# The offsets' 3x3 convolution in five matmuls a piece, with the third taps of two rows in one

## The chip, the cores and the metric

The kernel runs on one core of one Trainium2 chip. The metric is the device time of one execution in microseconds (us), as the median of several runs.

## What is computed

The input is 8 images of 64 channels and 16 x 16 pixels. Two residual blocks follow one another; the second is where the change lies.

```python
x = x + _L0_conv_ref(_gn(x), ...)      # 3x3 average pool, local 3x3 attention, gate, projection
x = x + _L1_conv_ref(_gn(x), L1_conv_w_om, L1_conv_b_om, L1_conv_w_dcn)

def _L1_conv_ref(x, w_om, b_om, w_dcn):            # DG, K = 4, 3
    om = conv_general_dilated(x, w_om, (1, 1), ((1, 1), (1, 1))) + b_om   # 3x3, 64 -> 108 channels
    o1, o2, mask = jnp.split(om, 3, axis=1)
    offset = jnp.concatenate([o1, o2], axis=1)
    mask = jax.nn.sigmoid(mask)
    return jax.nn.relu(_mdcn(x, offset, mask, w_dcn))   # bilinear samples at 9 shifted taps, x mask, x w_dcn
```

`_gn` is a group norm over pairs of channels. The convolution that is changed is `om`: for each pixel and each of nine taps it gives, for four channel groups, a mask and an offset in y and in x.

## The kernel before

**Layout.** Two halves of four images each lie on the partitions: half 0 on partitions 0 to 63 (64 channels), half 1 on 64 to 127, and along the free axis four images of 256 pixels. The first block (attention) fills the time to about 53 us; then come the second group norm's statistics, the convolution for the offsets, and the sampling, which runs over 72 steps (8 images x 9 taps).

**The convolution.** For each half there is a buffer, `dup[0]` and `dup[1]`, with four images padded to 18 x 18. Its lower 64 partitions hold the image, its upper 64 the same image moved by one column. So one matmul over 128 rows does two of the three taps of a row of the 3 x 3 stencil (kx 0 and 1), and another, with zero weights in the upper half, does the third (kx 2). With three rows that makes `TAPSTEPS` = 6 matmuls for a piece. There are five pieces: pieces 0 and 1 are one image slot each (256 columns, fp32), pieces 2, 3 and 4 two slots each (512 columns); pieces 0 to 2 read half 0, pieces 3 and 4 half 1. `convolve(p, k)` (L1139) issues step k of piece p; the last step signals `s_conv`.

**After a piece.** ACT's `offsets(p)` (L563) adds the bias (L568) and takes a tanh of the mask rows (L570). DVE's `offset_part` cuts the result into three bf16 parts (L849 to L857), and DMAs from SP (and for piece 0's x rows from POOL, L436) bring the parts to the stacks. From the stacks PE chooses rows: `select_y` (L1200), `select_x` (L1214), the masks (L1183, L1189). ACT makes distances and hats from these (L591, L596, L604, L606), DVE and POOL the low parts of the y hats (`low_y`), PE spreads them (L1229), DVE multiplies (L888) and PE takes the products (L1255).

**Order around the convolution.** Each engine has one hand-written order. DVE writes `dup[0]` image by image (L682, eight instructions, `s_dup0`), then `tall` (four, `s_tall`), a taller copy of all images from which the sampling windows are staged (`stage`, L834). PE does all of pieces 0 and 1 and three steps of piece 2, the first choices and windows, the rest of piece 2 between them, then the sampling. There, in image 0, each of the taps 0 to 5 carries one step of piece 3, and in image 3 taps 4 and 5 carry four and two steps of piece 4. ACT does `offsets(0)`, `second_half` (L555: two copies that fill `dup[1]` from `tall`), `offsets(1)`, then a queue of distances, hats and window copies up to `offsets(2)` (L626 to L636). POOL clears buffers at the start, works for the attention, issues the three DMAs of L436, and does `low_y` for the sampling. SP issues the loads of all constants at the start, the convolution's weights `womt` (L346) as the fourth.

Of the kernel before, what the change touches and what calls it, by code (L numbers as in the profile page):

```python
# [5 lines left out]
B, C, H, W = 8, 64, 16, 16  # L6
# [31 lines left out]
CHUNKS = 3  # L38
TC = TAPS // CHUNKS
CONV = [0, 1, 2, 3]  # L40
TAPSTEPS = 6
POOL_TAPS = 3


# [64 lines left out]
def bass_local_attention_then_deformable_conv(nc, x, cf, wom, sel16, rows16, out):  # L109
# [8 lines left out]
    with ExitStack() as ctx:  # L118
# [3 lines left out]
        def sem(name):  # L122
            return ctx.enter_context(nc.semaphore(name))
# [56 lines left out]
        window_words = sb("windows_attention", [P, max(len(PAIRROWS) * P + 2 * MSLOT, sum(n for _, n in ATT))])  # L180
        v = views(window_words, *ATT)
        pooled, q, chans, hidden, counts, shares, kpad, hsum, gate, att, vpad, dlog, lmax, den = (v[k] for k, _ in ATT)
        v = views(window_words, ("xs", len(PAIRROWS) * P), ("masks", 2 * MSLOT))
        xs, masks = v["xs"], v["masks"]

# [105 lines left out]
        s_dve = sem("s_dve")  # L291
        s_x2, s_x2seq = sem("s_x2"), sem("s_x2seq")
        s_tall, s_dup0, s_dup1 = sem("s_tall"), sem("s_dup0"), sem("s_dup1")
        s_conv, s_omraw, s_om, s_parts = (sem(n) for n in ("s_conv", "s_omraw", "s_om", "s_parts"))
        s_stack = {k: [sem(f"s_{k}stack{n}") for n in range(len(PIECES))] for k in "xym"}
        s_amaxed = sem("s_amaxed")
# [44 lines left out]
        @block.sync  # L341
        def _(sp):
            for c in range(2):
                sp.dma_start(xin[:, c * BANK:(c + 1) * BANK], x[:, c * BANK:(c + 1) * BANK]).then_inc(s_x[c], 16)
            sp.dma_start(bcast[:, 2 * DG * P:], sel16["bcast"][:, 3 * DG * P:]).then_inc(s_bcast, 16)
            sp.dma_start(womt[:, :], wom).then_inc(s_wom, 16)  # L346
            sp.dma_start(selx[:, :].bitcast(u16), sel16["selx"]).then_inc(s_selxd, 16)
            sp.dma_start(bcast[:, 0:2 * DG * P], sel16["bcast"][:, DG * P:3 * DG * P]).then_inc(s_byd, 16)
            sp.dma_start(sely[:, :].bitcast(u16), sel16["sely"]).then_inc(s_sel, 16)
            for k in range(3):  # L350
                for a in range(2):
                    sp.dma_start(selm[:, k * P + a * C:k * P + (a + 1) * C].bitcast(u16).rearrange("p (d c) -> p d c", d=DG),
                                 mask_columns(sel16["selm"], 3 * a + k)).then_inc(s_sel, 16)
                sp.dma_start(selm[:, 3 * P + k * C:3 * P + (k + 1) * C].bitcast(u16).rearrange("p (d c) -> p d c", d=DG),
                             mask_columns(sel16["selm"], 6 + k)).then_inc(s_sel, 16)
            for k in "xym":
                sp.dma_start(stack[k][STACK:STACK + 2, :].bitcast(u16), rows16["x" if k == "x" else "y"]).then_inc(s_rows, 16)

            sp.wait_ge(s_x2, 2)
            for h in range(HALVES):  # L360
                sp.dma_start(x2seq[:, :].rearrange("c (j h n) -> c j h n", j=J, h=HALVES)[:, :, h, :],
                             images(x2)[h * C:(h + 1) * C]).then_inc(s_x2seq, 16)

            for p, piece in enumerate(PIECES):
                for i in range(3):
                    sp.wait_ge(s_parts, 3 * p + i + 1)
                    sp.dma_start(*sent("y", piece, i)).then_inc(s_stack["y"][p], 16)
                for i in range(3):
                    if p:
                        sp.dma_start(*sent("x", piece, i)).then_inc(s_stack["x"][p], 16)  # L370
                for i in range(3):
                    if p:
                        whole = (piece[0], 0, BANK)
                        sp.dma_start(*sent("m", whole, i)).then_inc(s_stack["m"][p], 16)
            for i in range(B):
                sp.wait_ge(s_y, i + 1)
                sp.dma_start(in_order(out, i), result[:, i * HW:(i + 1) * HW]).then_inc(s_out, 16)
            sp.wait_ge(s_out, 16 * B)
            sp.wait_ge(s_choice, 1)
            passes = sp.value_load(choice[0:1, 0:1], min_val=1, max_val=SHIFTS)  # L380
            with sp.If(passes > 1):
                for i in range(B):
                    sp.wait_ge(s_y, B + i + 1)
                    sp.dma_start(in_order(out, i), result[:, i * HW:(i + 1) * HW]).then_inc(s_out, 16)
                sp.wait_ge(s_out, 2 * 16 * B)

        @block.gpsimd
        def _(pool):
# [4 lines left out]
            nc.gpsimd.memset(wb[:, :], 0.0).then_inc(s_wzero, 1)  # L393
            nc.gpsimd.memset(dup[0], 0.0).then_inc(s_zero, 1)
            nc.gpsimd.memset(dup[1], 0.0).then_inc(s_zero, 1)

            pool.wait_ge(s_zero, 6)
            pool.wait_ge(s_eps, 1)
# [35 lines left out]
            for i in range(3):  # L434
                pool.wait_ge(s_parts, i + 1)
                pool.dma_start(*sent("x", PIECES[0], i)).then_inc(s_stack["x"][0], 16)  # L436

            def stage(j, shift):

# [40 lines left out]
        def _(act):  # L480
# [70 lines left out]
            for c in range(2):  # L551
                high, _ = parts_at(c)
                nc.scalar.copy(halves[c][high, TAPS * HF:], den[high]).then_inc(s_rhi, 1)

            def second_half():  # L555

                act.wait_ge(s_tall, J)
                act.wait_ge(s_zero, 6)
                source = images(tall)[C:P, :, -FIRST_ROW * W:(-FIRST_ROW + H) * W].rearrange("p j (r c) -> p j r c", r=H)
                nc.scalar.copy(shifted(dup[1], 4)[0:C], source).then_inc(s_dup1, 1)  # L560
                nc.scalar.copy(shifted(dup[1], 3)[C:P], source).then_inc(s_dup1, 1)
# [46 lines left out]
            def sampling(it):  # L608
                for t in range(T):
# [13 lines left out]
                    if (i, m) == (LAST_CONV, 5) and isinstance(it, int):  # L623
                        offsets(4)

            offsets(0)  # L626
            second_half()
            offsets(1)
            distance_y(0, 0, 0)
            hat_x(0, 0)  # L630
            window_out(0, 0, 2)
# [367 lines left out]
        def _(pe):  # L999
# [139 lines left out]
            def convolve(p, k):  # L1139

                n, lo, hi = PIECES[p]
                h, j = n // 2, n % 2 * 2 + lo // HW
                ky, single = divmod(k, 2)
                if k == 0:
                    if h == 0:
                        pe.wait_ge(s_dup0, n % 2 * 2 + hi // HW)
                    else:
                        pe.wait_ge(s_dup1, 2)
                ins = nc.tensor.matmul(bank(CONV_BANK[p])[0:OM, lo:hi], womt[:, k * OM:(k + 1) * OM],  # L1149
                                       shifted(dup[h], 3 * ky + 2 * single)[:, j:j + (hi - lo) // HW], start=(k == 0),  # L1150
                                       stop=(k == TAPSTEPS - 1), skip_group_check=True)
                if k == TAPSTEPS - 1:
                    ins.then_inc(s_conv, 1)
# [169 lines left out]
            def sampling(it):  # L1323
                for t in range(T):
# [26 lines left out]
                    if i == LAST_CONV and m in (4, 5) and isinstance(it, int):  # L1351
                        if m == 4:
                            pe.wait_ge(s_vals, VALS * i)
                        for n in range(4) if m == 4 else (4, 5):
                            convolve(4, n)
                    if m in SEL_Y and i + 1 < B:
                        bank7_free(i, m, it)
# [20 lines left out]
                    block_of_products(B - 1, *LATE[m], it)  # L1378
                final(B - 1, it)

            pe.wait_ge(s_wom, 16)
            for p in range(2):
                for k in range(TAPSTEPS):
                    convolve(p, k)
# [18 lines left out]
            pe.wait_ge(s_absy, 2)  # L1403
            select_y(0, 2, 0)
            convolve(2, 4)
            convolve(2, 5)
            windows_out(0, 0)
            windows_out(1, 0)
            pe.wait_ge(s_wfin, 8)
# [124 lines left out]
```

## Time and profile before

| | us |
|---|---|
| median of 3 runs | 203.86 (203.85 to 203.88) |
| the profiled execution | 204.06 |
| its span on the core | 202.1 |

| engine | busy us | share of the span | instructions |
|---|---|---|---|
| PE (matmul) | 180.4 | 89% | 1806 |
| DVE | 160.8 | 80% | 268 |
| ACT | 106.5 | 53% | 199 |
| POOL | 84.6 | 42% | 103 |

Busy time counts an engine's instructions, not its waits for semaphores. The granted clock of TensorE was 0.998 of full over the execution. All times below are from the start of the span.

### The profile page before, as it was taken

The numbers are of one execution on the slowest core, as the hardware profiler recorded it, in microseconds if no ns is written. First come the engines' busy times: TensorE is split into PE (matmuls) and PEld (weight loads), VectorE is DVE, ScalarE is ACT, GpSimd is POOL, SyncE is SP. The second block draws the span as 40 slices with busy tenths as digits, with TensorE's granted clock in tenths as the row PEclk, the third lists the DMA queues.
The fourth block names the chain that finished last, engine by engine and source line by source line (L and its number), as shares of the span: only waits on it lengthen the run. The fifth ranks groups of instructions, "written<-read, shape, count | busy, mean of one in ns | idle before, by whom it ended". The sixth has DMA issues, their size and how long they took to land.

```text
span 202.1 us, 4583 instructions
## 1 busy us (share of the span) xinstructions
PE 180.4 (89%) x1806; PEld 125.7 (62%) x1806; DVE 160.8 (80%) x268; ACT 106.5 (53%) x199; POOL 84.6 (42%) x103
## 2 busy tenths in 40 slices
PE   0398996979989989999998999999979999999990
PEld 0234954644347535457787789638757788998870
DVE  0899868994859778987999888725999898999931
ACT  1136147600006796569757778726855878877000
POOL 8336962766023073205705607500842725626000
PEclk9999999999999999999999999999999999999999
DMA  6940000000040110010001000000002100000000
GB/s 185 340 33 2 3 0 0 3 0 0 0 104 11 29 31 7 12 51 0 11 24 40 0 3 0 3 0 0 12 18 61 37 2 16 0 16 2 19 0 23
DMA packets 8500, 5.55 MB, mean 27 GB/s; under 512 B 4887, under 2 KB 7461, under 8 KB 8473
## 3 DMA queue, kind: packets, MB, share of 16 engines
q1 hardware_dynamic: 8089, 4.25, 8.1%
q10 hardware_dynamic: 288, 0.89, 1.4%
q8 instruction: 16, 0.26, 0.5%
q14 instruction: 11, 0.09, 0.1%
q0 software_dynamic: 96, 0.06, 0.1%
HBM read 2.82 MB, written 0.52 MB: 17 GB/s over the span
## 4 chain that ended last, share of the span: by engine, by line
PE 65%; DVE 17%; ACT 7%; issue 4%; DMA 3%; POOL 2%; SPq 0%; DVEq 0%; POOLq 0%
PE ps L1255 19%; PE ps L1229 11%; PE ps L1149 9%; PE ps L1045 4%; PE ps L1166 4%; DVE smp_prod L777 3%; PE ps L1214 3%; DMA x_parts<-in_x 3%; PE ps L1297 3%; PE ps L1082 3%; DVE smp_prod L888 3%; PE ps L1303 3%; PE ps L1200 2%; PE ps L1183 1%; ACT haty L596 1%
## 5 line engine op out<-in xcount | busy, mean ns | idle before, releaser
L888 DVE TENSOR_TENSOR smp_prod<-ps,hx_selx 128x768 f32<-128x768 f32 x72 | 67.0, 952 | 8.7 <-PE ps L1229 7.9
L1255 PE MATMUL ps<-smp_prod,windows_attention 128*64 128x192 f32 (+2 forms) x512 | 54.3, 336 | 0.0
L1255 PEld LDWEIGHTS ps<-smp_prod,windows_attention 128*64 128x64 f32 x512 | 38.5, 136 | 5.3 <-ACT windows_attention L575 0.3
L451 POOL TENSOR_SCALAR disty<-disty 64x512 f32<-64x512 f32 (+1 forms) x23 | 12.6, 547 | 65.5 <-ACT haty L596 65.4
L1229 PE MATMUL ps<-haty,by_rows 128*64 128x256 f16 x432 | 38.0, 274 | 2.0 <-DVE smp_prod L888 1.8
L1229 PEld LDWEIGHTS ps<-haty,by_rows 128*64 128x64 f16 x432 | 25.2, 109 | 7.8 <-DVE smp_prod L888 3.8
L604 ACT ACTIVATE hx_selx<-ps 128x512 f32<-128x512 f32 x36 | 21.3, 592 | 14.1 <-PE ps L1214 13.8
L458 POOL TENSOR_TENSOR haty<-disty,haty 64x512 f16<-64x512 f32 (+1 forms) x23 | 24.0, 1045 | 1.9
L1149 PE MATMUL ps<-conv_staged 128*108 128x512 f32 (+1 forms) x60 | 23.3, 521 | 0.7 <-ACT x_parts L568 0.7
L606 ACT ACTIVATE hx_selx<-hx_selx 128x512 f32<-128x512 f32 x36 | 22.7, 630 | 1.1
L591 ACT ACTIVATE disty<-ps 128x512 f32<-128x512 f32 (+1 forms) x24 | 12.5, 521 | 8.7 <-PE ps L1200 8.1
L902 DVE TENSOR_TENSOR vals_attw<-ps,windows_attention 128x384 f32<-128x384 f32 x24 | 13.3, 553 | 4.6 <-PE ps L1255 3.0
L1214 PE MATMUL ps<-stack_x,selx 110*64 110x256 bf16 x144 | 15.4, 272 | 0.0
L454 POOL TENSOR_SCALAR disty<-disty 64x512 f32<-64x512 f32 (+1 forms) x23 | 14.1, 612 | 1.9
L1149 PEld LDWEIGHTS ps<-conv_staged 128*108 128x108 f32 x60 | 9.5, 172 | 8.0 <-issue 6.0
L582 ACT COPY windows_attention<-ps 128x512 f32<-128x512 f32 (+1 forms) x24 | 11.3, 469 | 5.6 <-PE ps L1183 3.3
L596 ACT ACTIVATE haty<-disty 128x512 f16<-128x512 f32 (+1 forms) x24 | 13.4, 559 | 0.8
L568 ACT ACTIVATE x_parts<-ps,kept 108x256 f32<-108x256 f32 (+1 forms) x3 | 1.6, 540 | 22.1 <-PE ps L1149 22.1
L422 POOL TENSOR_TENSOR smp_prod<-smp_prod 128x1024 f32<-128x1024 f32 x4 | 9.4, 2354 | 6.0 <-DVE smp_prod L777 6.0
L1082 PE MATMUL ps<-smp_prod,kept 128*128 128x512 f32 x20 | 9.6, 611 | 1.6 <-POOL smp_prod L422 1.6
L777 DVE TENSOR_TENSOR smp_prod<-ps,windows_attention 128x1024 f32<-128x1024 f32 x9 | 10.5, 1211 | 0.1
L1214 PEld LDWEIGHTS ps<-stack_x,selx 110*64 110x64 bf16 x144 | 9.5, 110 | 0.0
(140 smaller groups left out, 274.3 us busy)
## 6 DMA issues: line engine op xcount, KB each, us to landing
x_parts<-in_x SPq DMA_DIRECT2D x2, 256.0 KB, 5.3
bcast<-in_bcast SPq DMA_DIRECT2D x2, 256.0 KB, 6.7
x2seq<-x_parts SPq DMA_DIRECT2D x2, 256.0 KB, 3.8
out<-x_parts SPq DMA_DIRECT2D x8, 64.0 KB, 2.2
vals_attw<-in_cf ACTq DMA_DIRECT2D x1, 480.0 KB, 5.9
stack_m<-x_parts SPq DMA_DIRECT2D x12, 36.0 KB
kept<-in_cf ACTq DMA_DIRECT2D x1, 390.5 KB, 4.4
conv_staged<-in_wom SPq DMA_DIRECT2D x1, 324.0 KB, 6.8
```

Source lines behind the costliest of these rows:

```text
L454: nc.gpsimd.tensor_scalar(d, d, -1.0, 1.0, ALU.add, ALU.mult).then_inc(s_uy, 1)
L458: nc.gpsimd.tensor_tensor(hi, d, hi, ALU.add).then_inc(s_loy, 1)
L596: nc.scalar.activation(haty[i % 2][:, YP[e] * HW:YP[e] * HW + w], d, ACT.Relu, bias=1.0, scale=-1.0).then_inc(s_hiy, 1)
L604: nc.scalar.activation(h, bank(5), ACT.Abs).then_inc(s_absx, 1)
L606: nc.scalar.activation(h, h, ACT.Relu, bias=1.0, scale=-1.0).then_inc(s_hatx, 1)
L777: nc.vector.tensor_tensor(grid(prod[:, t * N:(t + 1) * N]), grid(bank(PB[pos % 3], 2)), shifted(vpad, t), ALU.mult).then_inc(s_pv, 1)
L888: nc.vector.tensor_tensor(pairs, rows, cols.unsqueeze(1).to_broadcast([P, QUARTERS, HW]), ALU.mult).then_inc(s_mult, 1)
L1082: ins = nc.tensor.matmul(bank(2 + c), ident, prod[:, t * N + c * BANK:][:, 0:BANK], start=(t == 0), stop=(t == 6))
L1149: ins = nc.tensor.matmul(bank(CONV_BANK[p])[0:OM, lo:hi], womt[:, k * OM:(k + 1) * OM], shifted(dup[h], 3 * ky + 2 * single)[:, j:j + (hi ...
L1214: ins = nc.tensor.matmul(bank(5)[h * C:(h + 1) * C, k * HW:(k + 1) * HW], selx[:, tap * P + h * C:tap * P + (h + 1) * C], stack["x"][:, i ...
L1229: ins = nc.tensor.matmul(ps[h * C:(h + 1) * C, at:at + HW], by_matrix(a, QUARTERS - 1 - k)[:, h * C:(h + 1) * C], haty[i % 2][:, p * HW:(p ...
L1255: return nc.tensor.matmul(dst[:, at:at + strips * 3 * SP].rearrange("p (s k n) -> p s k n", k=3, n=SP), rows, sampled(i, ki, m, first, str ...
```

## The change

Per piece five matmuls are issued instead of six. Steps 0 to 2 are the pairs of taps of the three rows, step 3 is the third tap of the last row as before, and step 4 does the third taps of the first and the second row in one matmul. For it there is, per half, a second copy of the images, `thirds[h]`: in its lower partitions the image moved by one column and one row down, in its upper partitions moved by one column only, with zeros in the last column and, in the lower half, the first row.

`thirds[0]` lies in the last 1024 words of an existing buffer and is filled by ACT from `dup[0]`, two copies an image, for images 0 and 1 before `offsets(0)` and for 2 and 3 behind it; `offsets(1)` now comes before `second_half`. `thirds[1]` is a new buffer, filled by POOL with two copies from `tall`, behind its three DMA issues. POOL clears the border zeros with four memsets at the start. The weights come in five DMAs instead of one. In image 0 piece 3 now takes taps 0 to 4, in image 3 piece 4 takes three and two steps.

```diff
-TAPSTEPS = 6
+TAPSTEPS = 5
+WOM = [0, 2, 3, 4, 1]
...
+        rows_words = sb("rows_words", [P, J * HW])
+        thirds = [window_words[:, window_words.shape[1] - J * HW:], rows_words]
...
+        s_third, s_tzero = [sem(f"s_third{h}") for h in range(HALVES)], sem("s_tzero")
...
-            sp.dma_start(womt[:, :], wom).then_inc(s_wom, 16)
+            sp.dma_start(womt[:, 0:OM], wom[:, 0:OM]).then_inc(s_wom, 16)
+            for half in range(2):
+                sp.dma_start(womt[half * C:(half + 1) * C, OM:2 * OM],
+                             wom[0:C, (1 + 2 * half) * OM:(2 + 2 * half) * OM]).then_inc(s_wom, 16)
+            sp.dma_start(womt[:, 2 * OM:3 * OM], wom[:, 2 * OM:3 * OM]).then_inc(s_wom, 16)
+            sp.dma_start(womt[:, 3 * OM:5 * OM], wom[:, 4 * OM:6 * OM]).then_inc(s_wom, 16)
...
+            for h in range(HALVES):
+                nc.gpsimd.memset(grid(thirds[h])[:, :, :, W - 1:W], 0.0).then_inc(s_tzero, 1)
+                nc.gpsimd.memset(grid(thirds[h])[0:C, :, 0:1, 0:W - 1], 0.0).then_inc(s_tzero, 1)
...
+            pool.wait_ge(s_tall, J)
+            for part in range(2):
+                rows = H - 1 + part
+                source = images(tall)[C:P, :, -FIRST_ROW * W:(-FIRST_ROW + rows) * W].rearrange("p j (r c) -> p j r c", r=rows)
+                nc.gpsimd.tensor_copy(grid(thirds[1])[part * C:(part + 1) * C, :, 1 - part:H, 0:W - 1],
+                                      source[:, :, :, 1:W]).then_inc(s_third[1], 1)
...
+            def third_taps(j):
+
+                act.wait_ge(s_dup0, j + 1)
+                source = shifted(dup[0], 4)[0:C, j]
+                for part in range(2):
+                    nc.scalar.copy(grid(thirds[0])[part * C:(part + 1) * C, j, 1 - part:H, 0:W - 1],
+                                   source[:, 0:H - 1 + part, 1:W]).then_inc(s_third[0], 1)
...
+            act.wait_ge(s_tzero, 2)
+            third_taps(0)
+            third_taps(1)
             offsets(0)
+            third_taps(2)
+            third_taps(3)
+            offsets(1)
             second_half()
-            offsets(1)
...
-                ins = nc.tensor.matmul(bank(CONV_BANK[p])[0:OM, lo:hi], womt[:, k * OM:(k + 1) * OM],
-                                       shifted(dup[h], 3 * ky + 2 * single)[:, j:j + (hi - lo) // HW], start=(k == 0),
+                if k == 4:
+                    pe.wait_ge(s_tzero, 4)
+                    pe.wait_ge(s_third[h], 2 if h else 2 * (n % 2 * 2 + hi // HW))
+                    rows = grid(thirds[h])
+                else:
+                    rows = shifted(dup[h], 3 * k if k < 3 else 8)
+                ins = nc.tensor.matmul(bank(CONV_BANK[p])[0:OM, lo:hi], womt[:, WOM[k] * OM:(WOM[k] + 1) * OM],
+                                       rows[:, j:j + (hi - lo) // HW], start=(k == 0),
...
-                        for n in range(4) if m == 4 else (4, 5):
+                        for n in range(3) if m == 4 else (3, 4):
...
-            pe.wait_ge(s_wom, 16)
+            pe.wait_ge(s_wom, 16 * 5)
...
             convolve(2, 4)
-            convolve(2, 5)
```

## Rows read from the trace of the kernel before

**Rows 1.** Page, busy shares; table by stretches, 67.4 to 74.9: busy us by engine
```profile
PE 180.4 (89%) x1806; PEld 125.7 (62%) x1806; DVE 160.8 (80%) x268; ACT 106.5 (53%) x199; POOL 84.6 (42%) x103
...
67.40:74.90 7.50, 6.83 (x54) 3.78 (x53) 6.12 (x10) 6.96 (x14) 3.19 (x3) 1.00 0.11 31
```

**Rows 2.** Chain of waits: start us, us, engine, tile and line
```profile
59.51 7.98 PE ps L1149 x30
67.75 0.39 ACT disty L591
...
74.24 0.58 ACT x_parts L568
...
86.25 1.04 PE ps L1149 x2
...
130.50 3.61 PE ps L1149 x8
```

**Rows 3.** Timeline, weight loads, from 130 us: start, us, engine, line, out<-in, [idle before]
```profile
130.95 0.17 PEld L1149 LDWEIGHTS ps<-conv_staged 128*108 128x108 f32 x1 [0.26 <-issue]
131.38 0.17 PEld L1149 LDWEIGHTS ps<-conv_staged 128*108 128x108 f32 x1 [0.26 <-issue]
```

**Rows 4.** ACT, timeline 62 to 65.5; groups by form (busy us, mean ns)
```profile
62.35 0.48 ACT L568 ACTIVATE x_parts<-ps,kept 108x256 f32<-108x256 f32 x1 [22.05 <-PE ps L1149]
62.86 0.42 ACT L570 ACTIVATE x_parts<-x_parts 36x256 f32<-36x256 f32 x1
...
64.47 1.06 ACT L561 COPY conv_staged<-tall 64x1024 f32<-64x1024 f32 x1
...
L553 ACT CAST haty<-windows_attention 64x128 f16<-64x128 f32 x2 | 0.6, 297 | 1.4 <-DVE windows_attention L789 1.4
```

**Rows 5.** DVE, timeline from 58.5; table by stretches (DMA share, GB/s last)
```profile
58.53 3.41 DVE L682 TENSOR_SCALAR conv_staged<-x_parts,pair,rstd 64x256 f32<-64x256 f32 x8 [1.14 <-POOL rstd L432]
...
61.98 1.38 DVE L682 TENSOR_SCALAR tall<-x_parts,pair,rstd 128x256 f32<-128x256 f32 x4
...
66.80:66.90 0.10, 0.10 (x2) 0.00 (x0) 0.07 (x2) 0.00 (x0) 0.00 (x0) 1.00 0.28 67
```

**Rows 6.** POOL, timeline 63 to 72; group by form of its cast
```profile
63.91 1.81 POOL L436 DMA_DIRECT2D stack_x<-x_parts x3 [5.42 <-DVE x_parts L849]
71.54 0.61 POOL L451 TENSOR_SCALAR disty<-disty 64x512 f32<-64x512 f32 x1 [5.82 <-ACT haty L596]
...
L417 POOL CAST haty<-windows_attention 64x384 f16<-64x384 f32 x3 | 1.6, 531 | 2.6 <-ACT windows_attention L530 2.6
```

**Rows 7.** Timeline 66 to 78: DVE, PE, ACT and POOL
```profile
66.51 0.29 DVE L849 CAST x_parts<-x_parts 108x256 bf16<-108x256 f32 x1 [0.39 <-ACT x_parts L570]
...
68.69 0.29 DVE L866 TENSOR_SCALAR disty<-disty 64x256 f32<-64x256 f32 x1 [0.64 <-ACT haty L596]
...
70.20 0.50 PE L1229 MATMUL ps<-haty,by_rows 128*64 128x256 f16 x6
...
72.51 0.57 ACT L575 COPY windows_attention<-ps 128x512 f32<-128x512 f32 x1
...
76.56 1.16 POOL L458 TENSOR_TENSOR haty<-disty,haty 64x512 f16<-64x512 f32 x1
...
77.06 0.95 DVE L849 CAST x_parts<-x_parts 108x512 bf16<-108x512 f32 x1
```

**Rows 8.** Timeline 87 to 94: ACT and DVE behind piece 3's last step
```profile
87.67 0.59 ACT L582 COPY windows_attention<-ps 128x512 f32<-128x512 f32 x1 [1.82 <-PE ps L1183]
...
88.70 0.96 DVE L888 TENSOR_TENSOR smp_prod<-ps,hx_selx 128x768 f32<-128x768 f32 x1 [0.72 <-PE ps L1229]
...
93.25 0.56 DVE L902 TENSOR_TENSOR vals_attw<-ps,windows_attention 128x384 f32<-128x384 f32 x1 [1.46 <-ACT windows_attention L582]
```

**Rows 9.** Timeline, DVE behind the burst of piece 4
```profile
134.61 0.96 DVE L888 TENSOR_TENSOR smp_prod<-ps,hx_selx 128x768 f32<-128x768 f32 x1 [3.10 <-PE ps L1229]
```

**Rows 10.** Timeline, POOL before the first norm: start, us, what, [idle before, releaser]
```profile
10.35 1.36 POOL L399 TENSOR_TENSOR rstd<-vareps,minushalf 128x4 f32<-128x4 f32 x1 [3.69 <-DVE vareps L679]
```

More of the change, by code:

```diff
@@ L1142, in convolve @@
                 h, j = n // 2, n % 2 * 2 + lo // HW
-                ky, single = divmod(k, 2)
                 if k == 0:
```

## The prediction

> **What bounds the kernel now.** I first read the busy shares: TensorE (PE) works 89% of the span, DVE 80%, ACT 53% [rows 1]. Such shares mix stages, so the chain of waits comes next, for the places where the offsets' convolution (L1149) runs. It shows three: 7.98 us of L1149 from 59.51, then ACT alone from 67.75 until its third bias step ends at 74.82; then one PE step after another with an L1149 in each tap (the last one at 86.25); and 3.61 us of L1149 at 130.50 [rows 2]. The table by stretches confirms the gap between the first two: there ACT is full, 6.96 of 7.5 us [rows 1]. So a convolution step taken away is worth its time in the second and third place, and in the first only as far as ACT gets started earlier.
>
> **What is removed.** A step is an fp32 matmul in two passes (30 passes for the first 15 steps [rows 2]). A pass of 512 columns takes 0.43 us, the distance of two weight loads in the burst at 130 [rows 3]; one of 256 half, 0.215. As a check, the first run is 24 passes of 256 and 6 of 512: 5.16 + 2.58 = 7.74, and the last has to drain, against 7.98. Six steps become five: 0.43 us less in each of pieces 0 and 1, 0.86 in each of 2, 3 and 4, 3.44 us of PE in all. What of it reaches the end is worked out place by place.
>
> **Place 1, the prologue (59.5 to 74.9).** Piece 0 is handed over 0.43 us earlier: ACT's bias step moves from 62.35 to 61.92 [rows 4]. But ACT has eight copies (64 partitions, 225 or 240 elements) besides. Their price c: its copy of 128 elements took 0.30 us, its step over 256 elements 0.42, its copy of 1024 1.06 [rows 4]. Interpolated between the first two, c = 0.39; ends for the range 0.30 and 0.53, half of the last. That last one already writes rows padded from 16 to 18, so I see no price for short rows.
> The first four copies start with the images: DVE finishes one every 0.85 us from 58.53 [rows 5], so they run from about 59.4 to 61.1, where ACT sat idle (22.05 us before 62.35). PE reaches the fifth step of piece 0 at 59.51 + 8 x 0.215 = 61.2 and of piece 1 at 63.4, behind the copies (60.3 and 61.1): its two new waits hold nothing up. Were they late, the other pieces and the first choices of rows (L1200) are queued behind them. The other four copies stand between the bias steps of pieces 0 and 1: 61.92 + 0.93 (L568, L570) + 4 x 0.39 = 64.41, when piece 1 is ready (64.1). Then piece 1's two, 0.93; then the second half's two copies, 2.15, which now come behind them. ACT is free at 67.49, and its unbroken queue, which began at 67.75, begins **0.26** earlier. It can't begin much sooner: DVE is busy writing `tall` until 63.36 and cuts the first parts no earlier than before, so the packets of the stacks for L1200, still moving at 66.8 [rows 5], come no earlier; with L1200 behind them the floor is 0.4 earlier. With c = 0.53 the sum gives 0.30 later. The rest of PE's gain here (0.43 + 0.43 + 0.86) is lost: it waits longer for ACT's third bias step (ends at 74.82) before piece 3. Piece 3 is also the first reader of the moved second half, long done by then.
>
> **POOL's two copies** (900 and 960 elements) come behind its three DMA issues, which end at 65.72, and ahead of its step at 71.54, for which it idled 5.82 us [rows 6]. By that step (0.61 us for 512) they take 2.2 together, by its 384-element cast (0.53) 2.6: done by 68.4. Piece 3's fifth step, past 82, reads them. Cost on POOL nil; without those idle 5.8 us `low_y` and L1229 behind it would be late.
> But a row speaks against it: DVE's cast at 77.06 took 0.95 us; POOL's add beside it ended at 77.72, and the cast 0.29 later, the whole of an undisturbed (half as wide) cast [rows 7]. It had waited 0.66. Two such collisions cost 1.3 us. DVE's parts of piece 1 can start at 66.12 instead of 66.51, and there is 0.64 idle before `low_y` at 68.69 [rows 7]: 1.03 of it is covered, and 0.3 later `low_y` still serves the windows that ACT copies out at 72.51. So nil. The other end: DVE stands still all through both copies, 2.6 us; 1.6 is then left, L1229 (70.2 now) slips to 71.8 and four transposes stand between it and ACT's copy, which then starts near 72.8 instead of 72.25: 0.55 later, place 1 a loss of 0.3.
> The Trainium skill's page "SBUF — State Buffer", section "Who interferes with whom", rules for the second end: DVE and GpSimd share a port pair, and the instruction that comes second blocks until the other is over. The 0.95 of the cast agrees with it. By it the sum below would be 1.56 instead of 2.12.
>
> **Place 2, piece 3 inside image 0.** PE does one step of it with each tap; the sixth goes. From its start to the mask's matmuls behind it is 1.04 us [rows 2], more than its 0.86. Behind it stand the mask, four transposes and the rows of tap 7, all about 1 us earlier. ACT waited 1.82 us for that mask, so it follows in full. DVE gets only 0.72, its idle time before the product at 88.70; but at 93.25 it waits 1.46 us for ACT's mask copy anyway [rows 8]. What is last there is ACT, earlier by **1.0**. Ends: 0.7 (if DVE is) and 1.04.
>
> **Place 3, the burst in image 3.** Eight passes become six, **0.86** us. DVE idles 3.10 us until PE comes through [rows 9], so nothing of the gain is caught there. Ends: 0.7 and 0.9.
>
> **The start.** SP issues five weight transfers instead of one. Four more push the constants behind them, which POOL and PE read much later; the convolution reads its weights at 59.5 [rows 2], and the images are issued ahead of them. POOL's four small memsets (60 or 64 elements) lie before a wait of 3.69 us [rows 10]: nil up to 0.9 us each. Ends: 0 and 0.1.
>
> **Sum.** 0.26 + 1.0 + 0.86 = 2.12 us. The profiled execution took 204.06 (span 202.1 and 1.96 around it), so 201.94; the median of the runs, 203.86, is 0.20 lower, and by that 201.74, say **201.7**.
>
> **Rivals.**
> 1. Every removed pass counts: 3.44 less, 200.4. For it: PE is full in all three places. Against: ACT's unbroken queue from 67.75. Chance 0.05.
> 2. The second end of POOL's copies: place 1 loses 0.3, 1.56 less, 202.3; if besides DVE is last in place 2 (0.7), 202.6. For it: DVE's 0.95 [rows 7]. Against: ACT's queue has to be hit exactly, and 2.1 us of standstill still leave it whole. Chance 0.22.
> 3. It doesn't do what it says: image 0 gains nothing and the prologue loses what the burst gains, within 0.4 of 203.86. Against: ACT and DVE both wait for PE there [rows 8, 9]. Chance 0.06.
> 4. Slower: ACT's copies are dear. Once c exceeds 0.62 the first four end after 61.92, and ACT's queue begins at 59.45 + 8c + 0.93 + 0.93 + 2.15 = 63.46 + 8c. Against the 1.86 gained elsewhere that breaks even at c = 0.77 and is 0.4 slower from 0.82; at the 1.06 of the 1024-element copy 4.19 - 1.86 = 2.3 slower, 206.2. For it: fifteen rows of 15 elements instead of one run. Against: the padded copy's price [rows 4]. Chance 0.04.
> The forecast, 201.2 to 202.1, has 0.63.
>
> **How the numbers follow.** The range reaches towards rival 1 at the low end (0.5 more of the prologue and of place 2 than I take), and at the high end takes in rival 2 and some of 3: 200.9 to 203.0, leaving out about 0.15. A measurement of this kernel tells some 0.2% (0.4 us) from no change. Faster holds the forecast, 1 and 2, almost whole: 0.89; same 0.06; slower 0.05.
>
> **What the changed profile would show.** 50 passes of L1149; eight ACT copies near 0.39, four of them before 61.9; L591 starting ACT's queue near 67.5; piece 3's first pass near 74.6; the mask of tap 5 one step earlier; the burst with six passes and DVE's wait there near 2.2. I would be wrong if the copies exceed 0.53, if DVE's casts beside POOL push the first L1229 past 71.5, or if DVE, not PE, paces image 0.

## The result and the profile after

The changed kernel took 202.08 us (median of four runs, 201.94 to 202.56) against 203.86 on the same chip: a ratio of 0.992, 95% interval 0.9901 to 0.9938, or 1.78 us less (1.26 to 2.02). Forecast were 201.7 and a range of 200.9 to 203.0. Faster, and inside the range, but 0.3 us of the 2.12 are missing at the median, and more in the profile.

The profiled execution of the changed kernel took 202.56 us with a span of 200.3. The first lines are those of its page: busy us, share of the span and instructions of each engine, then the group of ACT's new copies (busy us, mean ns, idle before).

```profile
PE 177.5 (89%) x1796; PEld 124.4 (62%) x1796; DVE 162.0 (81%) x268; ACT 109.4 (55%) x207; POOL 86.8 (43%) x109
...
L582 ACT COPY windows_attention<-conv_staged 64x225 f32<-64x225 f32 (+1 forms) x8 | 3.1, 385 | 19.3 <-DVE conv_staged L717 19.1
```

PE loses 2.9 us of busy time and ACT gains 2.9; the span falls by 1.8. Where it fell shows in the chain of waits of the changed kernel (start us, us, engine, tile and line). The convolution is now L1189, the distances L621, the bias step L598, the choice of y rows L1240; they stood at L1149, L591, L568 and L1200.

```profile
7.18 0.76 DVE halfstat L700 x2
...
65.15 2.38 DMA stack_y<-x_parts
...
75.11 1.11 PE ps L1189 x2
...
84.07 1.04 PE ps L1189 x2
...
88.15 1.03 PE ps L1295 x8
...
129.76 2.76 PE ps L1189 x6
...
196.05 0.42 DVE x_parts L956
```

The same places in the chain of the kernel before, where the rows don't have them:

```profile
7.33 0.77 DVE halfstat L665 x2
...
74.86 1.11 PE ps L1149 x2
...
88.89 1.03 PE ps L1255 x8
...
197.66 0.42 DVE x_parts L921
```

One thing has to be taken out first: the head, the time up to the first statistics. The second transfer of the images lands at another time in every execution: in the profiles below its entry in the chain is 5.77 to 6.36 us long, and all that follows is shifted by that. Six profiles of kernels that don't differ up to there have 5.77 to 6.29, so I don't put it down to the change. I count from the first statistics behind it (7.18 us here, 7.33 before) to the start of the last DVE operation: 188.87 us after, 190.33 before, **1.46 less**. By the same count:

- ACT's unbroken queue (67.75 before [rows 2], 67.99 after) starts **0.39 later**, and piece 3's first pass 0.40 later (74.86, now 75.11).
- Image 0 takes **0.99 less** from there to the products behind piece 3 (L1255 at 88.89 before, L1295 at 88.15 after; 0.25 later has become 0.74 earlier).
- The burst of piece 4 takes **0.85 less** (3.61 [rows 2], now 2.76).

0.40 - 0.99 - 0.85 = -1.44: the three places hold the whole difference. Two gave what was forecast; the prologue, forecast as a gain of 0.26, lost 0.4. So the question for the experiments is what became of the prologue, where PE does 1.72 us less. This is its timeline in the changed kernel: start, us, engine, line, operation, out<-in, count, [idle before, what ended it].

```profile
59.29 1.62 ACT L582 COPY windows_attention<-conv_staged 64x225 f32<-64x225 f32 x4 [19.13 <-DVE conv_staged L717]
61.76 0.47 ACT L598 ACTIVATE x_parts<-ps,kept 108x256 f32<-108x256 f32 x1 [0.86 <-PE ps L1189]
...
62.59 1.61 ACT L582 COPY windows_attention<-conv_staged 64x225 f32<-64x225 f32 x4
...
65.56 2.19 POOL L457 COPY rows_words<-tall 64x900 f32<-64x900 f32 x2
65.83 1.03 DVE L884 CAST x_parts<-x_parts 108x256 bf16<-108x256 f32 x1
66.25 1.06 ACT L591 COPY conv_staged<-tall 64x1024 f32<-64x1024 f32 x1
66.90 1.13 DVE L887 TENSOR_TENSOR x_parts<-x_parts 108x256 f32<-108x256 f32 x1
67.66 0.30 PE L1240 MATMUL ps<-stack_y,s_sely 110*64 110x256 bf16 x2 [1.20 <-DMA stack_y<-x_parts]
...
67.99 0.38 ACT L621 ACTIVATE disty<-ps 128x256 f32<-128x256 f32 x1 [0.68 <-PE ps L1240]
...
68.93 0.29 DVE L901 TENSOR_SCALAR disty<-disty 64x256 f32<-64x256 f32 x1
...
75.11 1.11 PE L1189 MATMUL ps<-conv_staged 128*108 128x512 f32 x2 [1.53 <-ACT x_parts L598]
```

ACT is done with everything at 66.25 + 1.06 = 67.31 and then idles 0.68 us. What it waits for is L1240, and PE waited 1.20 us before that for the transfer of the y stacks, which the chain has landing at 65.15 + 2.38 = 67.53. Counted the same way, these stacks landed at 67.22 before, by the record of the increments of its semaphore. DVE's cast and subtraction beside POOL's copies took 1.03 and 1.13 us, but `low_y` (L901) still came right behind ACT's hat at 68.93.

### The profile page after: what moved, and what is told of

Same layout as the page of the kernel before. It is cut to its first block, busy times and chain, and to the rows that moved or that the text cites. A ratio compares the mean times of both kernels' runs of the same rounds, so it can differ in the third digit from the quotient of the medians.

```text
span 200.3 us, 4587 instructions
## 1 busy us (share of the span) xinstructions
PE 177.5 (89%) x1796; PEld 124.4 (62%) x1796; DVE 162.0 (81%) x268; ACT 109.4 (55%) x207; POOL 86.8 (43%) x109
## 3 DMA queue, kind: packets, MB, share of 16 engines
HBM read 2.76 MB, written 0.52 MB: 16 GB/s over the span
## 4 chain that ended last, share of the span: by engine, by line
PE 61%; DVE 18%; ACT 7%; issue 5%; DMA 4%; POOL 2%; SPq 0%; DVEq 0%
PE ps L1295 19%; PE ps L1269 10%; PE ps L1080 4%; PE ps L1189 3%; PE ps L1206 3%; DVE smp_prod L812 3%; DMA x_parts<-in_x 3%; PE ps L1254 3%; PE ps L1337 3%; PE ps L1117 3%; DVE smp_prod L923 3%; PE ps L1063 3%; PE ps L1343 3%; PE ps L1240 2%; DVE conv_staged L717 2%
## 5 line engine op out<-in xcount | busy, mean ns | idle before, releaser
L923 DVE TENSOR_TENSOR smp_prod<-ps,hx_selx 128x768 f32<-128x768 f32 x72 | 66.9, 952 | 6.4 <-PE ps L1269 5.7
L1295 PE MATMUL ps<-smp_prod,windows_attention 128*64 128x192 f32 (+2 forms) x512 | 54.3, 336 | 0.0
L1295 PEld LDWEIGHTS ps<-smp_prod,windows_attention 128*64 128x64 f32 x512 | 38.5, 136 | 5.3 <-ACT windows_attention L605 0.3
L1189 PE MATMUL ps<-conv_staged 128*108 128x512 f32 (+1 forms) x40 | 16.0, 521 | 1.6 <-ACT x_parts L598 1.5
L621 ACT ACTIVATE disty<-ps 128x512 f32<-128x512 f32 (+1 forms) x24 | 12.5, 521 | 8.1 <-PE ps L1240 7.5
L582 ACT COPY windows_attention<-conv_staged 64x225 f32<-64x225 f32 (+1 forms) x8 | 3.1, 385 | 19.3 <-DVE conv_staged L717 19.1
L1240 PE MATMUL ps<-stack_y,s_sely 110*64 110x256 bf16 x80 | 9.3, 277 | 1.2 <-DMA stack_y<-x_parts 1.2
L1189 PEld LDWEIGHTS ps<-conv_staged 128*108 128x108 f32 x40 | 6.3, 172 | 6.4 <-issue 3.9
```

What stands on the lines that cost most here:

```text
L923: nc.vector.tensor_tensor(pairs, rows, cols.unsqueeze(1).to_broadcast([P, QUARTERS, HW]), ALU.mult).then_inc(s_mult, 1)
L1295: return nc.tensor.matmul(dst[:, at:at + strips * 3 * SP].rearrange("p (s k n) -> p s k n", k=3, n=SP), rows, sampled(i, ki, m, first, str ...
```

## The experiments

Twelve kernels, in the order of the questions. "End" is the count above (first statistics to last DVE operation) against the 190.33 of before; "queue" is the start of ACT's first distances by the same count.

| kernel | median us | before, same chip | ratio (95%) | end, us | queue |
|---|---|---|---|---|---|
| before, profiled | | | | 0 | 60.42 |
| changed, profiled | 202.08 | 203.86 | 0.992 (0.9901 to 0.9938) | -1.46 | 60.81 |
| after_again | 202.41 | 203.93 | 0.9945 (0.9925 to 0.9966) | -1.27 | 60.98 |
| short_p1 | 203.52 | 203.93 | 0.9989 (0.9974 to 1.0003) | -0.12 | 60.31 |
| short_p2 | 202.93 | 203.93 | 0.995 (0.9934 to 0.9967) | -0.99 | 60.43 |
| short_p3 | 203.19 | 203.93 | 0.9967 (0.9951 to 0.9982) | -0.88 | 60.41 |
| late_pool | 203.60 | 203.96 | 0.9986 (0.9972 to 1.0) | -0.49 | 60.98 |
| two_memsets | 203.00 | 203.96 | 0.9948 (0.9934 to 0.9962) | -1.28 | 60.99 |
| early_bias | 202.13 | 203.96 | 0.9908 (0.9894 to 0.9922) | -2.34 | 60.83 |
| both | 202.02 | 203.96 | 0.9905 (0.9891 to 0.9919) | -2.07 | 61.08 |
| before_pad9 | 203.95 | 203.84 | 1.0008 (0.9996 to 1.002) | +0.03 | 60.45 |
| before_pad7 | 203.45 | 203.80 | 0.999 (0.9975 to 1.0005) | 0.00 | 60.42 |
| merged_pair | 202.07 | 203.84 | 0.9921 (0.9904 to 0.9938) | -1.37 | 60.89 |
| merged_bias | 201.08 | 203.84 | 0.9871 (0.9852 to 0.989) | -2.25 | 60.89 |

Medians and ends part by up to 0.5 us: the medians contain the head, and they come from several executions, an end from the profiled one alone. Where a difference is under 0.5 us I go by the end and the queue, and each of these is one profile. Times of packets and landings in the expectations stand on an axis that runs 0.24 us ahead of the page's.

**after_again: the changed kernel once more.**

> The changed kernel once more, unaltered. In its first profile the choice of rows (L1240) waited 1.20 us for the stack of y to land, and the last of that transfer's sixteen parts came 0.44 us after the others, beside an instruction fetch of 8 KB on a DMA engine. Theory A (place 1 gives nothing because the landing of the stacks gates ACT's queue, fetch or not): ACT's L621 starts near 67.5 to 67.6 without the fetch, at most 0.2 us earlier than before's 67.75, and the median stays near 202.05. Theory B (the fetch alone ate place 1's 0.26): without it L621 starts by 67.3 and the time is below 201.8.

202.41 us, with an end of -1.27 and the queue at 60.98. So the late queue is no accident of the first profile: 0.39 and 0.56 late in the two. The fetch was there again too (at 66.41), so this run can't tell A from B.

**short_p1, short_p2, short_p3: the sixth step left out in one place at a time**, from the kernel before, with no copies. The edit of short_p1 (the list is [5, 5, 5, 4, 5] in short_p2 and [5, 5, 5, 5, 4] in short_p3):

```diff
+LAST_STEP = [4, 4, 4, 5, 5]
-                                       stop=(k == TAPSTEPS - 1), skip_group_check=True)
-                if k == TAPSTEPS - 1:
+                                       stop=(k == LAST_STEP[p]), skip_group_check=True)
+                if k == LAST_STEP[p]:
```

Those steps are not issued either, so these kernels leave out one tap in the pieces named.

> The kernel before with the sixth step of pieces 0, 1 and 2 left out (the third tap of the last row is missing there), no copies, nothing else: what PE's 1.72 us in place 1 are worth alone. Theory A (ACT's queue there is gated by the landing of the stacks, and PE's time isn't on the path): 0 to 0.2 us less than before, 203.7 to 203.86. Theory B (PE's time counts once no copies stand in ACT's way): 0.4 us or more less.

> The kernel before with the sixth step of piece 3 left out (the third tap of the last row is missing in images of that piece), no copies. My sum's step for place 2: 1.0 us less than before, 202.86; if DVE limits there, 0.7 less, 203.16; if the step were off the path, none.

> The kernel before with the sixth step of piece 4 left out (the third tap of the last row is missing in images of that piece), so the burst in image 3 has six passes and four, no copies. My sum's step for place 3: 0.86 us less than before, 203.0; if the gain is caught by another queue later, less than 0.5.

short_p2 ends 0.99 earlier and its median is 1.0 us lower; short_p3 0.88 and 0.74. In the chain of short_p3 the burst is the changed kernel's to the hundredth:

```profile
130.48 2.76 PE ps L1150 x6
```

short_p1 is the surprise. It takes 1.72 us of PE out of the prologue, adds nothing to ACT, and ends 0.12 earlier. (Its median is 0.41 lower, but the ratio of the runs, 0.9974 to 1.0003, is not clear of 1.) Its chain says why:

```profile
7.34 0.76 DVE halfstat L666 x2
...
65.31 1.86 DMA stack_y<-x_parts
...
67.65 0.39 ACT disty L592
```

The y stacks land at 67.17 and ACT's queue starts 0.48 behind, at 67.65. PE is there before them and waits 0.68 us. Even with copies that cost nothing the prologue could bring 0.1, because the stacks land no earlier. The three together make 1.99; the changed kernel lacks 0.5 to 0.7 of that, all of it in the prologue.

**late_pool: POOL's two copies moved** behind its second `low_y`, to 78 us, so that nothing of POOL runs beside DVE's casts at 66.

```diff
-            pool.wait_ge(s_tall, J)
-            for part in range(2):
...
                 for e in range(1, 3):
                     low_y(0, e, it)
+                if isinstance(it, int):
+                    pool.wait_ge(s_tall, J)
+                    for part in range(2):
...
```

> The changed kernel with POOL's two copies behind the low parts of image 0's y hats, near 78 us, instead of near 65.6. There DVE's casts and subtractions of piece 1 lose their stall (in the profile 1.03 and 1.13 us for 0.29 and 0.43), and the copies meet DVE's full stretch from 77 to 88. Theory A (the stall costs nothing at 66 us, what is late is the landing beside the fetch): with only the four memsets ahead the fetch falls near 64 us, the landing is on time, L621 starts near 67.5, 0.45 earlier; but the copies then hold DVE up by 1 to 2 us in its full stretch: in all 0.5 faster to 1 slower than the changed kernel. Theory B (the stall at 66 us is what delays the prologue): L621 and the first L1269 start 0.4 or more earlier.

The queue starts at 60.98, as late as in after_again: POOL's copies and DVE's standstill at 66 us aren't the cause of the late stacks, and B falls. A's fetch near 64 and its punctual queue didn't come either: the fetch lay at 66.36. And the kernel lost 0.8 to 1.0 us of what the changed kernel has (1.2 to 1.4 by the medians). DVE has idle time to catch the standstill at 66 us and none at 79. These are POOL and DVE in late_pool:

```profile
78.36 2.06 POOL L484 COPY rows_words<-tall 64x900 f32<-64x900 f32 x2
...
79.50 1.47 DVE L889 TENSOR_TENSOR x_parts<-x_parts 108x512 f32<-108x512 f32 x1
...
83.15 0.68 DVE L910 COPY windows_attention<-ps 128x512 f32<-128x512 f32 x1
```

and the same two DVE operations in the changed kernel:

```profile
79.15 0.68 DVE L887 TENSOR_TENSOR x_parts<-x_parts 108x512 f32<-108x512 f32 x1
...
82.01 0.68 DVE L908 COPY windows_attention<-ps 128x512 f32<-128x512 f32 x1
```

late_pool enters this stretch 0.35 later (its distances start at 68.34 against 67.99). The subtraction takes 0.79 longer, and the copy of windows that PE's next products wait for comes 1.14 later, which is 0.79 more than that head start. So the price of POOL's copies is real, and the changed kernel doesn't pay it because they lie where DVE has room.

**early_bias: the third bias step ahead of the distances of tap 2 in ACT's queue.** In the changed kernel PE idles 1.53 us for that step (L598) before piece 3, and it stands behind work that only a later tap needs.

```diff
-            distance_y(0, 2, 0)
             offsets(2)
+            distance_y(0, 2, 0)
```

> The changed kernel with ACT's bias step of piece 2 (offsets(2)) ahead of the third distance of image 0 (distance_y(0, 2, 0)) instead of behind it. Theory A (what PE gained in place 1 was lost to ACT's order: piece 2 is ready at 72.9 since it has one step less, but ACT comes to it at 74.38): L598 starts near 73.3, piece 3's first pass near 74.0 instead of 75.11, and as DVE waits for PE there (1.5 us before its copy of the windows), about 1 us less than the changed kernel. Theory B (something else, POOL's low part at 75.3 or DVE from 77 on, limits at once): less than 0.3 us less.

```profile
7.61 0.76 DVE halfstat L700 x2
...
68.44 0.40 ACT disty L621
...
73.77 0.60 ACT x_parts L598
74.41 1.11 PE ps L1189 x2
...
195.60 0.42 DVE x_parts L956
```

ACT's queue starts as late as before this edit (60.83), and yet piece 3 begins at 66.80 from the first statistics, 1.13 earlier than in the changed kernel (67.93), and the end is 0.9 to 1.1 earlier. The medians of the two kernels, taken on different chips, don't show it (202.13 against 202.08 and 202.41). Two pairs below that differ by this order alone, each on one chip, do: `both` against two_memsets 202.02 and 203.00, merged_bias against merged_pair 201.08 and 202.07, by the ends 0.79 and 0.88. This is where PE's gain in the prologue had gone: PE had it, and then waited for an ACT step that nothing forced to be so late.

**two_memsets and both: the fetch.** The transfers show one more thing at 66 us. The view of DMA queues of the changed kernel, from 65 to 68 us (packets, MB, share of 16 engines; the last number of an issue is us to landing), has a packet of instructions:

```profile
q14 instruction: 1, 0.01, 0.6%
...
stack_x<-x_parts POOLq DMA_DIRECT2D x2, 18.0 KB, 2.0
```

The kernel before has none in that stretch (its own comes at 73.5), and there:

```profile
stack_x<-x_parts POOLq DMA_DIRECT2D x2, 18.0 KB, 1.7
```

It is 8 KB and starts at 66.20 in the changed kernel. Of the increments of the y stack's last transfer, all but one came by 67.08 and the last at 67.52 (67.73 in after_again); of the x stack's, 66.67 and 67.35. Before, all of the y stack's came by 67.22. So one part is late. It is the increment that is late: the last packet of these transfers ended at 66.70, and the view shows none of any kind from 66.75 to 67.6. One theory (A in the later expectations) was that the fetch makes it late; its rival (B) that ACT with its copies is simply full. If the fetch was POOL's, whose program had grown by six instructions, two fewer memsets should move it:

```diff
-                nc.gpsimd.memset(grid(thirds[h])[:, :, :, W - 1:W], 0.0).then_inc(s_tzero, 1)
-                nc.gpsimd.memset(grid(thirds[h])[0:C, :, 0:1, 0:W - 1], 0.0).then_inc(s_tzero, 1)
+                nc.gpsimd.memset(thirds[h][:, :], 0.0).then_inc(s_tzero, 1)
```

> The changed kernel with two memsets of the whole second copies on POOL instead of four of their borders: POOL's stream is two instructions shorter in front of the copies, nothing else differs. In both profiles of the changed kernel an 8 KB instruction fetch lies at 66.4 to 66.7 us, one of the sixteen parts of the last x and y transfers lands 0.4 to 0.8 us behind the others, and ACT's queue (L621) starts at 68.0 to 68.2; in the four profiles without the change's copies the fetch lies at 73.4 to 73.7 and nothing is late. Theory A (POOL's own instruction fetch, moved forward by its six more instructions, holds up a DMA engine): with two fewer the fetch moves to about 71 to 72 us, the stacks land by 67.3, L621 starts near 67.5, and the time is 0.4 to 0.6 us below the changed kernel's. Theory B (POOL's copies themselves, or DVE's stall beside them, make the transfers late): the landing stays late and the time the same. The larger memsets (about 0.9 us each) stay within POOL's wait of 3.2 us before the first norm.

> Two whole memsets and the early bias step together. Theory A for both: the gains add, 0.45 + 1.0, near 200.5 to 200.8 where the changed kernel has 202.1. If they are one and the same gain (both start piece 3 earlier, and POOL's low part at 75.3 limits what follows), no more than the larger of the two.

A missed in its form here. The fetch stayed (66.88, in a run whose head came 0.49 later), so it isn't POOL's, and the stacks were late by as much (queue 60.99). What did move with POOL's count is the next fetch (74.2 in the changed kernel, 74.8 in after_again, 76.3 here and 77.1 in `both`). For the same reason `both` missed A's 200.5 to 200.8 and brought nothing beyond early_bias: -2.07 against -2.34.

**before_pad9, before_pad7: nine or seven copies of one column on ACT, near 41 us, in the kernel before.** They lengthen ACT's program about as the eight copies do, and leave its work of the prologue as it was.

```diff
+            for n in range(9):
+                nc.scalar.copy(spare[:, n:n + 1], threehalf[:, :])
             offsets(0)
```

> The kernel before, with nine one-column copies on ACT in its idle time near 41 us and nothing else. In every profile with the change's copies so far an 8 KB instruction fetch lies at 66.4 to 67.1 us and one sixteenth of the last stack transfers lands 0.4 to 0.8 us late, even where POOL's copies are moved away or its stream is shorter; in the profiles without them it lies at 73.4 to 73.7. Theory A (it is ACT's fetch, moved forward by its nine more instructions, and it holds up a DMA engine): the fetch moves to about 66.5, L592 starts near 68.1 to 68.2 instead of 67.75, and the kernel is 0.3 to 0.5 us slower than before although it does no more work there. Theory B (the copies' own traffic delays the landing): no difference.

> The kernel before with seven one-column copies on ACT near 41 us instead of nine, and nothing else. With nine the 8 KB fetch moved from 73.7 to 64.7 us, so it is ACT's, but it came before the last stack transfers and held nothing up; in the kernels with the change's copies it came between 65.9 and 67.1 and part of those transfers was late each time. With seven it should come two ACT instructions later than with nine, near 66.3. Theory A (the fetch alone holds the transfers up): a sixteenth of the last transfer lands late, the wait in the chain is near 2.4 us instead of 1.9, L592 starts 0.2 to 0.4 us later than in the kernel before, and the time is as much longer. Theory B (the change's copies do it, the fetch only falls together with them): all parts land together and L592 starts near 67.75.

The fetch did move, from 73.5 to 64.5 and 64.7, so it belongs to ACT's stream. But it came ahead of the last transfers of the stacks, not among them, nothing was late, and no time was lost (queue 60.45 and 60.42, end +0.03 and 0.00). In the view of queues of before_pad9, from 64.2 to 65.2 us:

```profile
q14 instruction: 1, 0.01, 1.9%
...
stack_x<-x_parts POOLq DMA_DIRECT2D x2, 18.0 KB, 1.8
```

A's numbers missed in both. That a fetch nearby is enough to cost time is refuted; whether one at 65.7 to 66.9 does, these two can't tell, since neither put it there.

**merged_pair, merged_bias: less work for ACT.** The third copies of images 2 and 3 as two instructions of 450 and 480 elements instead of four; merged_bias with the order of early_bias besides.

```diff
+            def third_pair():
+                act.wait_ge(s_dup0, J)
+                for part in range(2):
+                    nc.scalar.copy(grid(thirds[0])[part * C:(part + 1) * C, 2:4, 1 - part:H, 0:W - 1],
+                                   shifted(dup[0], 4)[0:C, 2:4, 0:H - 1 + part, 1:W]).then_inc(s_third[0], 2)
...
-            third_taps(2)
-            third_taps(3)
+            third_pair()
```

> The changed kernel with the second copies of images 2 and 3 made together: two ACT copies of 450 and 480 elements instead of four, so ACT has three instructions fewer (one wait among them) and some 0.5 us less to do between piece 0's and piece 1's bias steps. Theory A (ACT's fetch): the fetch leaves the time of the stack transfers (towards 68 to 70 us), they land in full by 67.3, L621 starts at 67.5 to 67.6 and the time is 0.3 to 0.5 us below the changed kernel's. Theory B (ACT's queue is late because it is full): L621 starts earlier by the 0.5 us saved whatever the fetch does. If the fetch stays at 66.5, A expects no gain.

> The pair's copies merged as in the run before, and ACT's bias step of piece 2 ahead of the third distance as in the earlier run with the early bias. Theory A: the early bias gives about 0.9 us less than the changed kernel (it gave that by the profile), the merged pair 0.3 to 0.5 more if the fetch moves away: 200.7 to 201.0 against a kernel before at 203.9. If the fetch stays, as the early bias alone.

The two copies took 1.18 us instead of 1.61. ACT's idle time before its distances grew by nearly as much, from 0.68 to 1.07, and nothing came earlier. This is merged_bias, first its timeline, then its chain:

```profile
62.51 1.18 ACT L589 COPY windows_attention<-conv_staged 64x450 f32<-64x450 f32 x2
...
65.86 1.05 ACT L598 COPY conv_staged<-tall 64x1024 f32<-64x1024 f32 x1
67.98 0.38 ACT L628 ACTIVATE disty<-ps 128x256 f32<-128x256 f32 x1 [1.07 <-PE ps L1246]
```

```profile
7.09 0.76 DVE halfstat L706 x2
...
65.06 2.45 DMA stack_y<-x_parts
...
195.17 0.42 DVE x_parts L962
```

The stacks land at 67.51, ACT has been free since 66.91, and its queue starts at 60.89 as in the changed kernel (60.81 and 60.98). So B falls: ACT with 0.4 us more to spare is not earlier. A had said that nothing is gained if the fetch stays, and it stayed, at 65.7 and 65.8. merged_pair alone is worth nothing (202.07 us). merged_bias is the best version of all: **201.08 us, 0.9871 of before (0.9852 to 0.989)**, 2.76 us less, about 1 us better than the change as it was made. By its end (-2.25) it equals early_bias; for its lead of 1.05 at the median I have no full reading. The two profiled executions are 0.40 apart (201.70 and 202.10), which is less than their heads are (7.09 and 7.61), and the medians come from two chips.

**What stays open.** The late part is there in all eight profiles of kernels with the new copies (0.35 to 0.95 us behind the others) and in none of the six without. POOL's copies are excluded as its cause by late_pool, a full ACT as the cause of the late queue by merged_pair. But the eight with copies are also the eight with the fetch between 65.7 and 66.9, so here no run has one without the other.

The same traces have it at another place. Near 180 us one transfer of results leaves (64 KB), and a fetch of 16 KB falls close to it. These are the views of queues of the kernel before from 178.5 to 182.5 us and of the changed kernel from 176.5 to 180:

```profile
q8 instruction: 1, 0.02, 1.7%
...
out<-x_parts SPq DMA_DIRECT2D x1, 64.0 KB, 3.0
```

```profile
q8 instruction: 1, 0.02, 2.3%
...
out<-x_parts SPq DMA_DIRECT2D x1, 64.0 KB, 2.1
```

In all six kernels without the copies this fetch starts 0.8 to 1.6 us behind the issue, and the last of the sixteen increments comes 0.95 to 1.6 us behind the fifteenth. In all eight with the copies it starts 1.9 to 2.2 us behind the issue, when the packets are through, and the last increment comes 0.01 behind. So the late part goes with the fetch and not with the copies. It is the same over the fourteen traces from 20 us on, where I took the increments of one semaphore without a break of 1.8 us as a group (ten and more). Of 183 groups that had no fetch in the 1.5 us before their last increment but one, none had the last one more than 0.04 us late; of the 139 others 37 had it over 0.2 us late. A fetch nearby is therefore not enough. That it is what made the stacks late in the prologue is likely, and not shown: no run moved a fetch alone into their transfers. The Trainium skill's page "DMA: Bandwidth & Descriptors", section "Queues, rings and completion order", would join fetch and lateness: the increment of one of the sixteen engines lands only after every earlier write of that engine, across its queues. One late part fits that, but no run here shows which engine carried the fetch.

## Why the prediction held, and the step that failed

**Copies on ACT.** Taken at 0.39 each; measured 0.385. The working of ACT's queue was right throughout: by the count from the first statistics the first bias step started at 61.91 on before's axis (forecast 61.92) and ACT was free at 67.46 (forecast 67.49). Rival 4 is out.

**The prologue's floor is the step that failed.** I took the packets of the stacks, gone by 66.9 [rows 5], and let PE's choice of rows and ACT follow them 0.4 us earlier than before if ACT were ready. But the transfer counts as landed only with its last increment, at 67.22, some 0.3 behind the packets, and in the kernel before PE came to L1200 at 67.41, so that 0.19 was all there was to gain. short_p1 measures 0.1. The term of 0.26 should have been 0.1 to 0.2 from this alone. On top of it came what no row of before showed, one part of the last transfers 0.4 us and more late. In place of +0.26 the place gave -0.4. The 0.66 between the two is the whole difference between the forecast 2.12 and the profile's 1.46. The total came out inside the range because 1.86 of the 2.12 stood in the other two places; for place 1 even the sign was wrong.

**POOL's copies** took 2.19 us together (forecast 2.2). DVE did stand still: 0.74 us in the cast (1.03 instead of 0.29 [rows 7]) and 0.70 in the subtraction (1.13 instead of 0.43), 1.44 in all against a forecast of 1.3, and `low_y` came right behind ACT's hat as it was worked out. So nil was right. Rival 2's time, 202.3 with place 1 losing 0.3, is nearer to the measured 202.08 than the forecast's 201.7, and its 1.56 is nearer to the profile's 1.46 than 2.12, but that is luck: its mechanism, DVE at a standstill for 2.6 us, didn't come, and late_pool has no standstill there and the same late queue. In late_pool DVE's standstill behind POOL's copies did reach the end. The section "Who interferes with whom" of the Trainium skill's page "SBUF — State Buffer" has the second of two such instructions blocked until the first is over; the trace agrees (the cast 1.03 us instead of 0.29).

**The rest of PE's gain in the prologue** I wrote off, because PE would wait longer for the third bias step. It does, 1.53 us. What I didn't see is that most of this wait came from the order of ACT's queue: with that step ahead of one distance, early_bias has 0.38 of it left and ends 0.9 to 1.1 us earlier.

**Place 2**, forecast 1.0, gave 0.99, and 0.99 again alone. The reading that ACT is last there and DVE's 0.72 doesn't cap it [rows 8] held. In the changed kernel the mask's wait has shrunk from 1.82 to 0.67 and DVE's idle time before the product is gone; what is left is ACT, as before:

```profile
86.74 0.58 ACT L612 COPY windows_attention<-ps 128x512 f32<-128x512 f32 x1 [0.67 <-PE ps L1223]
...
92.51 0.56 DVE L937 TENSOR_TENSOR vals_attw<-ps,windows_attention 128x384 f32<-128x384 f32 x1 [1.29 <-ACT windows_attention L612]
```

**Place 3**, forecast 0.86, gave 0.85, and 0.88 alone. DVE's wait behind the burst was to fall from 3.10 [rows 9] to near 2.2:

```profile
133.01 0.96 DVE L923 TENSOR_TENSOR smp_prod<-ps,hx_selx 128x768 f32<-128x768 f32 x1 [2.25 <-PE ps L1269]
```

**The start** cost nothing that shows. POOL's four memsets took 0.17 to 0.23 each, and its wait before the norm is still 3.19 (3.69 [rows 10]).

**Rivals 1 and 3** are both refuted by the same runs: of 3.44 us of passes 1.84 counted, in two places of three.

The sum was 0.66 too high for the profiled run, and 0.34 and 0.60 by the two medians (1.78 and 1.52 us less than before).

## What to carry to other kernels

Where work is taken off an engine ahead of a transfer's landing, the floor is the landing, not the last packet: take it from the wait of the first reader, and ask whether that reader was already waiting. What an engine gains ahead of a queue that is full can still be had if the step it waits for can go first in that queue; look for this before the gain is written off. And a copy on GpSimd has a price that depends on the place: nothing beside a VectorE that idles, 0.8 us beside one that is full.

## What the runs showed of the hardware

- The y stack's transfer landed about 0.3 us behind the last packets (66.9 and 67.22). With a fetch of instructions in the 1.5 us before, the last increment of a transfer came 0.2 to 1.6 us behind the others in 37 groups of 139; without one it never came more than 0.04 us behind (183 groups).
- Instructions are fetched in packets of 8 and of 16 KB during the run (10 or 11 and 16 of them in one execution), beside the kernel's own transfers. Seven or nine more instructions on ACT moved one from 73.5 to 64.7 and 64.5 us; fewer instructions on POOL moved the next one from 74.2 to 76.3.
- GpSimd's copy also stretched VectorE's fp32 subtraction of two operands (0.43 to 1.13 us; 0.68 to 1.47 for 512 elements), not the cast alone, which was all that the kernel before had shown.
- The images' second transfer ended 5.77 to 6.29 us after the start of its entry in the chain, in six profiles of kernels that don't differ up to there: 0.5 us that look like an effect of an edit when two profiles are laid side by side.
